# Folding a layer norm into the products behind it: mean into the weights, factor into q, k and v, with a new prologue

## What is computed

```python
def _layernorm(x, axis=-1, eps=1e-05):
    m = jnp.mean(x, axis=axis, keepdims=True)
    v = jnp.var(x, axis=axis, keepdims=True)
    return (x - m) / jnp.sqrt(v + eps)
...
q = (x @ Wq + bq).reshape(b, s, NH, HD)
k = (x @ Wk + bk).reshape(b, s, NH, HD)
v = (x @ Wv + bv).reshape(b, s, NH, HD)
q = _layernorm(q, q_scale, q_bias)
k = _layernorm(k, k_scale, k_bias)
v = _layernorm(v, v_scale, v_bias)
scores = jnp.einsum('bqhd,bkhd->bhqk', q, k) * scale
probs = jax.nn.softmax(scores, axis=-1)
out = jnp.einsum('bhqk,bkhd->bqhd', probs, v).reshape(b, s, NH * HD)
return out @ Wo + bo
...
x = x + _L0_attn_ref(_layernorm(x, axis=-1), ...)
x = x + _L0_ffn_ref(_layernorm(x, axis=-1), ...)
```

## Time and profile before

| what | value |
|---|---|
| median of 3 runs | 345.06 us (344.67 to 345.42) |
| profiled execution, device time | 344.79 us |
| its span, first to last instruction | 343.0 us |
| TensorE busy | 311.4 us (91%), 4111 records |
| ScalarE (ACT) busy | 275.7 us (80%) |
| VectorE (DVE) busy | 234.0 us (68%) |
| POOL busy | 62.1 us (18%) |
| DMA traffic | 22.86 MB, mean 67 GB/s |

### The profile page before, as it was taken

How to read it: one execution, slowest core, us unless ns; L and a number is a source line. 1 busy time by engine, 2 the same in 40 slices (tenths; PEclk the granted TensorE clock), 3 DMA queues, 4 the chain that set the end, 5 groups by cost and what they waited for, 6 DMA issues and landing times.

```text
span 343.0 us, 10532 instructions
## 1 busy us (share of the span) xinstructions
PE 311.4 (91%) x4111; PEld 145.3 (42%) x4111; DVE 234.0 (68%) x609; ACT 275.7 (80%) x315; POOL 62.1 (18%) x110
## 2 busy tenths in 40 slices
PE   7588888899999999999999999999998998989997
PEld 7484332253353424452354335443442233323576
DVE  4886788777776877688677877787846462453255
ACT  1517989989987898889988998899889998999611
POOL 6752400311003200420012200420022100020020
PEclk9969999999999999999999999999999999999999
DMA  3624104224002320323023400232022203000000
GB/s 76 188 86 155 33 2 156 80 78 124 2 33 94 98 92 2 116 69 121 0 76 99 131 0 0 92 101 84 0 97 88 97 2 102 25 2 1 34 0 31
DMA packets 22948, 22.86 MB, mean 67 GB/s; under 512 B 3200, under 2 KB 19968, under 8 KB 22912
## 3 DMA queue, kind: packets, MB, share of 16 engines
q1 hardware_dynamic: 21200, 21.23, 19.5%
q10 hardware_dynamic: 1712, 1.15, 1.1%
HBM read 13.45 MB, written 8.65 MB: 64 GB/s over the span
## 4 chain that ended last, share of the span: by engine, by line
PE 54%; ACT 22%; issue 9%; DVE 9%; DMA 2%; ACTq 1%; POOL 1%; POOLq 0%; DVEq 0%
PE oacc L911 22%; ACT probs L765 20%; PE side L835 13%; PE side L828 8%; PE scores L896 8%; ACT osb L728 1%; DMA wraw<-in_L_attn_Wv 1%; DVE x2n L1085 1%; PE scores L1002 1%; DVE ht L1161 1%; DMA kst<-parts 1%; DVE qk_sum L1144 1%; DVE ht L1160 1%; DVE hy L1162 1%; ACT th L723 1%
## 5 line engine op out<-in xcount | busy, mean ns | idle before, releaser
L765 ACT ACTIVATE probs<-scores 128x1536 f32<-128x1536 f32 (+1 forms) x256 | 248.7, 1027 | 35.9 <-PE scores L896 33.8
L911 PE MATMUL oacc<-probs,vaug 128*32 128x512 f32 x1024 | 136.4, 604 | 7.2 <-ACT osb L728 3.4
L896 PE MATMUL scores<-qst,kst 32*128 32x512 f16 x512 | 50.5, 384 | 9.8 <-ACT probs L765 7.1
L560 POOL TENSOR_SCALAR ve<-mv 128x4 f32<-128x4 f32 (+1 forms) x17 | 9.0, 528 | 219.6 <-DVE mv L1079 198.5
L911 PEld LDWEIGHTS oacc<-probs,vaug 128*32 128x32 f32 x1024 | 20.3, 108 | 39.9 <-ACT probs L765 28.9
L835 PE MATMUL side<-x2T_parts,gu_parts 128*32 128x512 f16 x504 | 35.0, 379 | 1.3 <-DVE x2T_parts L1276 1.3
L896 PEld LDWEIGHTS scores<-qst,kst 32*128 32x128 f16 x512 | 12.9, 90 | 51.8 <-ACT probs L765 39.2
L835 PEld LDWEIGHTS side<-x2T_parts,gu_parts 128*32 128x32 f16 x504 | 14.3, 96 | 32.9 <-issue 22.3
L835 PEld LDWEIGHTS side<-wqkv,xnT 128*32 128x32 f32 x736 | 21.0, 110 | 14.3 <-issue 13.8
L835 PE MATMUL side<-wqkv,xnT 128*32 128x128 f32 x736 | 24.6, 273 | 1.7 <-DVE xnT L1106 0.9
L1282 DVE SCALAR_TENSOR_TENSOR ga<-th,side 128x512 f32<-128x512 f32 x21 | 14.4, 685 | 15.5 <-ACT th L723 15.5
(11 more groups left out here) (158 smaller groups left out, 346.3 us busy)
## 6 DMA issues: line engine op xcount, KB each, us to landing
parts_dram<-parts SPq DMA_DIRECT2D x15, 256.0 KB, 2.4
qst<-parts_dram SPq DMA_DIRECT2D x15, 256.0 KB, 2.7
kst<-parts_dram SPq DMA_DIRECT2D x15, 256.0 KB, 3.0
x_in<-in_L_attn_x SPq DMA_DIRECT2D x8, 256.0 KB, 2.6
x_res<-in_L_attn_x SPq DMA_DIRECT2D x8, 256.0 KB, 3.6
parts_dram<-parts SPq DMA_DIRECT2D x15, 128.0 KB, 1.9
out_dram<-y SPq DMA_DIRECT2D x7, 256.0 KB, 2.1
parts_dram<-shift_fill SPq DMA_DIRECT2D x2, 128.0 KB, 4.7
```

The lines of the kernel that those rows point to most:

```text
L560: pool.tensor_scalar(ve[:, ts], mv[:, ts, 1], LN_EPS, None, ALU.add).then_inc(ve_done, 1)
L765: act.activation(out, src, ACT.Exp).then_inc(exp_done, 1)
L896: last = pe.matmul(scores[:, j if j < TRIPLE else TRIPLE + u % 2, :], kst[r, g, kt * P:(kt + 1) * P], qst[r, g, :], start=True, stop=True)
L911: last = pe.matmul(oacc[STRIP * j:STRIP * (j + 1), :], vaug[:, kt, NG * g + j, :], probs[:, kt, j, :], start=first, stop=last_of_half)
```

## The change

The factor of the first norm and its mean are no longer applied to x. x is loaded a second time, already transposed by the host's layout (xT), and goes into the products as it is. The mean is taken out of the weights: (I - 1/128) W, and the heads' mean as well, both by two small products on TensorE per weight with copies on ScalarE in between. The norm's factor is applied where q, k and v are read out of PSUM: four operations of 128 columns with a per-row scalar, in place of one addition of 512 columns. The xT pieces, VectorE's copy and the application are gone. FFN weights come laid out transposed, and the nine transposes with their copies are gone. Small vectors are loaded together. The head norm's root is one third-order step and one Newton step, eight chained instructions after the seed where there were nine. In the prologue, POOL's clearing of vaug and its root of v move to VectorE, v_c of sequence 0 moves behind heads_normed, 26 keep_warm matmuls stand ahead of rq, and WARM_AGAIN is 36 instead of 12.

```diff
-WARM_AGAIN = 12
+WARM_NORM = 26
+WARM_AGAIN = 36
+W_KS = ([0], [1, 2])
-SIDE = {0: ["a_v"], 1: ["a_rq"], 2: ["b_OT1", "a_rk"], 3: ["b_onT", "e_xT"], 4: ["b_Wo"], ...
+SIDE = {0: ["a_v"], 1: ["a_rq"], 2: ["b_OT1", "a_rk"], 3: ["b_onT"], 4: ["b_Wo"], ...
-FIRST_SIDE = {1: ["f_xT"], 2: ["f_q"], 3: ["f_k"], 4: ["a_v"], 6: ["e_xT"], 8: ["a_rq"], ...
+FIRST_SIDE = {1: ["f_q"], 2: ["f_k"], 4: ["a_v"], 8: ["a_rq"], 9: ["a_rk", "e_q"], 10: ["e_k"],
...
+            def load_xT(b):
+                if not (isinstance(b, int) and b == 0):
+                    wait_apart(sp, v_filled, b, passed)
+                sp.dma_start(xT[:, :], xT_d[b, :, :]).then_inc(xT_loaded, 16)
...
                 wait_apart(pool, mv_done, NT * b + tiles[-1] + 1, passed)
+                if rs is rs1:
+                    wait_apart(pool, vc_done, b, passed)
...
+            def centred_weights():
+                for n, ks in enumerate(W_STEPS):
+                    act.wait_ge(w_mean_filled, n + 1)
+                    act.activation(wT_mean_out[:, ks, :], scores[:, n, 0:len(W_KS[n]) * P], ACT.Copy)\
+                       .then_inc(w_mean_copied, 1)
+                for n, ks in enumerate(W_STEPS):
+                    act.wait_ge(w_head_filled, n + 1)
+                    act.activation(wqkv[:, ks, :], scores[:, 2 + n, 0:len(W_KS[n]) * D], ACT.Copy).then_inc(w_centred, 1)
...
+            centre_weights()
             for k, (name, turn_before) in enumerate(PROLOGUE):
-                if k == 1:
-                    pe.wait_ge(w_centred, 1)
+                if name in ("e_q", "e_k"):
+                    pe.wait_ge(w_centred, 1 + k)
                 if name == "a_rq":
-                    prepare_later_weights()
+                    keep_warm(WARM_NORM, scores[:, 0, 0:P])
                 piece(name, turn_before, occupant_in_prologue(k))
-            pe.wait_ge(wT_copied, 3)
-            keep_warm(WARM_AGAIN, scores[:, 3, 0:P])
+            keep_warm(WARM_AGAIN, scores[:, 0, 0:P])
             output_bias_product()
...
+            def scaled_with_bias(b, out, bank, bias):
+                dve.wait_ge(rs1_done, b + 1)
+                for t in range(NT):
+                    last = dve.scalar_tensor_tensor(out=out[:, t, :], in0=bank[:, t * D:(t + 1) * D],
+                                                    scalar=rs1[:, t:t + 1], in1=wqkv[:, bias, :],
+                                                    op0=ALU.mult, op1=ALU.add)
+                return last
...
                 dve.wait_ge(sem_f, b + 1)
-                dve.tensor_tensor(out=qk_c[:, w, :, :],
-                                  in0=side[:, BANK[name], :].rearrange("p (t d) -> p t d", t=NT),
-                                  in1=wqkv[:, 3 + w, :].unsqueeze(1).broadcast_to((P, NT, D)), op=ALU.add)\
-                   .then_inc(qkc_done, 1)
+                scaled_with_bias(b, qk_c[:, w, :, :], side[:, BANK[name], :], 3 + w).then_inc(qkc_done, 1)
...
+            sums_cleared()
             ln1_stats(0)
-            centre_weights()
-            ln1_apply(0)
-            copy_xT(0)
             centre_biases()
...
             heads_normed(0)
-            sums_v(0)
+            centred_v(0)
+            prepare_small()
             dve.wait_ge(qk_aff_done, 2)
             own_parts()
-            prepare_small()
+            sums_v(0)
             score_bound()
+            own_v_rsqrts()
...
```

More of the change, by code:

```diff
@@ L95 @@
 IN_SUMS = ("a_v", 0)
-PROLOGUE = [("e_xT", -2), ("e_q", -2), ("e_k", -2), ("a_v", -1), ("a_rq", -1), ("a_rk", -1)]
+PROLOGUE = [("e_q", -2), ("e_k", -2), ("a_v", -1), ("a_rq", -1), ("a_rk", -1)]
 def slots_of(phase):
@@ L523, in turn @@
                     shift_rows(i)
+                if phase in ("first", "loop", "third last"):
+                    load_xT(i + 2)
                 if phase in ("first", "loop"):
@@ L536, in _ @@
                 turn(i, "loop")
-            turn(B - 3, "near")
+            turn(B - 3, "third last")
             turn(B - 2, "near")
@@ L802, in keep_warm, with centre_weights @@
                     pe.matmul(out, ident[:, :], ident[:, :], start=True, stop=True)
-            keep_warm(WARM_UP, scores[:, 3, 0:P])
-            def prepare_later_weights():
-                for m, w in enumerate((wg_f, wu_f, wd_f)):
-                    pe.wait_ge(ints_floated, m + 1)
-                    for j in range(NF):
-                        last = pe.transpose(scores[:, m, j * P:(j + 1) * P], w[:, j, :], ident[:, :])
-                    last.then_inc(wT_filled, 1)
+            keep_warm(WARM_UP, scores[:, 4, 0:P])
+            def centre_weights():
+                pe.wait_ge(filled, 8)
+                pe.wait_ge(w_loaded, 16)
+                for n, ks in enumerate(W_KS):
+                    for c, k in enumerate(ks):
+                        last = pe.matmul(scores[:, n, c * P:(c + 1) * P], w_raw[:, k, :], mean_out[:, :],
+                                         start=True, stop=True)
+                    last.then_inc(w_mean_filled, 1)
+                for n, ks in enumerate(W_KS):
+                    pe.wait_ge(w_mean_copied, n + 1)
+                    for c, k in enumerate(ks):
+                        last = pe.matmul(scores[:, 2 + n, c * D:(c + 1) * D], wT_mean_out[:, k, :], head_mean_out[:, :],
+                                         start=True, stop=True)
+                    last.then_inc(w_head_filled, 1)
             def output_bias_product():
@@ L1150, in _ @@
             n_qk = 2 * NT * NH
-            v_all, y_all, t_all = (z[:, :, :, :].rearrange("p w t h -> p (w t h)") for z in (hv, hy, ht))
+            v_all, y_all, t_all, a_all = (z[:, :, :, :].rearrange("p w t h -> p (w t h)") for z in (hv, hy, ht, ha))
             RUN_OF_QK = slice(0, n_qk)
-            def newton_step(run, k, cols):
-                def step(ins, n):
-                    ins.then_inc(newton, 1)
-                    dve.wait_ge(newton, 8 * run + 3 * k + n)
-                v, y, t = v_all[:, cols], y_all[:, cols], t_all[:, cols]
-                step(dve.tensor_tensor(out=t, in0=y, in1=y, op=ALU.mult), 1)
-                step(dve.scalar_tensor_tensor(out=t, in0=t, scalar=-0.5, in1=v, op0=ALU.mult, op1=ALU.mult), 2)
-                last = dve.scalar_tensor_tensor(out=y, in0=t, scalar=1.5, in1=y, op0=ALU.add, op1=ALU.mult)
-                if k < 2:
-                    step(last, 3)
-                else:
-                    last.then_inc(rsqrt_done, 1)
```

298 lines of the change are left out of this document (151 added, 147 removed).

## The result

The changed kernel takes 350.44 us (median of 4 runs, 350.03 to 350.72), the kernel before 345.24 beside it (4 runs, 344.67 to 345.60). The ratio is 1.0154, with a 95% interval of 1.0136 to 1.0173: slower, as forecast, but by 5.2 us where 2.5 were forecast, and outside the range of 345.3 to 349.8. The profiled execution took 350.72 us with a span of 349.0; its own span is 6.0 above the 343.0 of before.

What follows compares the result with a forecast made beforehand. It took data to bound the prologue, a 2.0 us floor per head unit turn 0, and mostly TensorE's work turns 1 to 5. Prologue +2.3, turn 0 +1.0 and loop -0.5 on 344.8 gave 347.6 us, range 345.3 to 349.8.

Steps and rivals of the forecast that it cites:

- The prologue, +2.3 forecast: Before turn 0: fillers in TensorE's queue move first scores from 27.2 to 29.5 us, +2.3 (bounds +1.6 and +3.5).
- at 26.1: Prologue: kst's data lands near 25.6, so without the fillers the scores could start at 26.1 us.
- Turn 0, +1.0 forecast: Turn 0: VectorE's added work makes qk_n late and a_rq passes it on, +1.0 us (bounds -0.7 and +1.9).
- the collision moves with the chain: Turn 0: POOL's FFN weight splitting starts later too, so it still slows the root's first steps (1.00 against 0.26).
- the clock at 1.00 throughout: Prologue sign of being right: unbroken TensorE fillers up to about 29 us, at the full granted clock.
- The factor sets, +0.26 forecast: Reading out q, k, v: four 128-wide operations take 0.95 against 0.69 us, +0.26 each (bounds +0.17 and +0.42).
- The loop, -0.5 forecast: Turns 1 to 5: removed transposes outweigh later x2T_parts, net -0.1 us a turn, -0.5 over five.
- VectorE runs without a gap: Turns 1 to 5: two of three set additions lie between Wo and x2T_parts, making x2T_parts 0.3 us later after Wo.
- Dear instructions: Rival, chance 0.15: factor sets cost +0.42 or more each, loop turns +0.25 instead of -0.1; run 349.5 us.
- No stall in turn 0: Rival, chance 0.12: POOL's splitting falls behind the root, 1.7 us of slowed steps and the stall go; run 345.9.
- The fillers don't bind: Rival, chance 0.06: prologue fillers cost at most half of 0.224, data sets the start at 26.1; run 344.2 us.
- TensorE's work is the price of the loop: Rival, chance 0.09: each loop turn gives back 0.60 and the wait, 4.0 us over five instead of 0.5; run 344.1.

Runs made afterwards that it cites:

- first experiment: Changed kernel with 16 fillers fewer (WARM_AGAIN 20 instead of 36): 349.79 us, ratio 1.0126 to the kernel before.
- fifth run: Changed kernel with the norm's factor left out, q, k and v read out by one wide addition instead of four operations: 346.51 us, ratio 1.0046.
- second experiment: Changed kernel with POOL's splitting of the FFN weights moved ahead of turn 0: 347.16 us, ratio 1.0065.
- third experiment: Changed kernel with the statistics of x for sequence 2 placed ahead of v's centring on VectorE: 347.25 us, ratio 1.007.
- fourth experiment: Changed kernel with ten fillers put ahead of a_rq in unit 8 of turn 0, inside TensorE's wait: 348.45 us, ratio 1.0105.
- ninth run: Changed kernel with VectorE's order in loop turns changed: centring before the second part of the x2 norm, squares later: 349.27 us, ratio 1.012.
- sixth experiment: Changed kernel with three fillers added in unit 3 of every loop turn: 353.66 us, ratio 1.0256.
- twelfth: Kernel before with VectorE's order in the loop turns changed, as in the ninth run: 344.91 us, ratio 1.0008.
- seventh run: Kernel before with POOL's splitting of the FFN weights moved ahead of turn 0's part: 346.25 us, ratio 1.0038.
- eighth: Changed kernel with 16 fillers fewer, POOL's FFN weight split before turn 0 and the statistics of x ahead of v: 345.33 us, ratio 1.0012.
- eleventh run: Changed kernel with 24 fillers, POOL's early weight split, statistics ahead of v and VectorE's new loop order: 343.40 us, ratio 0.9936.
- tenth: Changed kernel with 24 fillers instead of 36, POOL's early weight split and statistics ahead of v: 344.58 us, ratio 0.999.

## Why the prediction was wrong

**The prologue, +2.3 forecast, +3.13 measured.** The mechanism was right: fillers in TensorE's own queue, not the data (first experiment). The terms were too small by a few tenths each. The first 18 fillers end at 8.54 instead of 8.1; the weight products, put at 1.5 between bounds of 1.3 and 2.5, take 1.95 (10.49 - 8.54); q, k, v and the 26 fillers with 0.23 of wait end at 19.55 instead of 18.0. From there on the count of fillers held: 20.62 + 8.20 = 28.82. The 0.45 of issue that I added behind them isn't there. That the data "would be there" for scores "at 26.1" was wrong as well: with 16 fillers fewer it was 27.8, since kst's load was issued at 24.37 and not near 23.0, and took 3.10 and not 2.55. Part of the miss is chance: the same first fillers take from 5.70 to 7.11 us in the runs of the changed kernel and its variants, and the first scores of the seven kernels with this count of fillers start at 29.38 to 30.32, with the changed kernel's the latest. My 29.5 lies inside. In six of the seven they come 21.8 us behind the start of the weight products (21.2 in the fifth run), so this chance passes straight into the time. In the kernel before it doesn't: its first fillers took 5.68 to 6.79 in three kernels, and the first scores start at 27.17 to 27.19, since TensorE waits for data behind them. The change takes that wait away. I had reckoned with the 18 fillers as the bound of q, but gave their spread no price.

**Turn 0, +1.0 forecast, +3.86 measured.** This step failed, and it is the one that put the result outside the range.
- The lateness of qk_n: 21.52 after the first scores (51.84 - 30.32), where I had said 20.4. The sums started 1.93 later and not 1.46: v's product was ready 0.19 later (10.98 after the first scores for 10.79), the set took 0.29 more (1.04 for 0.75 from start to start), and the statistics 1.45 with a gap of 0.20 among them. And the sum and root together were 0.16 longer (7.21 for 7.05), not 0.4 shorter, because "the collision moves with the chain" was not the whole of it: it grew from 1.7 to 2.4, as v's squares on POOL joined it, and that outweighed the 0.5 that the shorter chain of steps gave. I had the squares in a bound (+1.9) and left them out of the forecast. Second and third experiment. In units 8 and 9 the lateness costs 1.9 (fourth experiment).
- The clock, **1.5 us**, was in no term and in no rival; I had written of the clock for the prologue alone ("the clock at 1.00 throughout") and asked nothing of it in turn 0. Yet the rows were there: behind the 2.60 of idle time in the earlier trace rows the transposes took 1.94, and the earlier trace rows has the clock at 0.50 there. A forecast wait of 0.91 + 1.0 = 1.9 should have raised the question. In the fourth experiment fillers in the stall gave back 1.5.
- The rest is 0.4: 0.2 in units 0 to 7, where the pieces are spread otherwise, and 0.2 in unit 11, which waits 0.41 for k's dearer set and doesn't in the fifth run.

**The factor sets, +0.26 forecast, +0.43 measured.** I took the value between a start distance of 0.19 and the two-scalar operation at 0.28 each, "because there is one scalar". The far end was right: 1.12 for four, as the earlier trace rows shows for the old apply, and over the 1.1 that I had named as a sign of being wrong. The row of 0.19 was of an operation on SBUF without a tensor as a second input, and so the poorer match. The Trainium skill, VectorE: DVE Perf Modes, section "The DRAIN you can't avoid", from which I had worked out the estimate of +0.47, was nearer than my reading; this case's trace agrees with it to 0.04.

**The loop, -0.5 forecast for five turns, -0.94 measured**, but for a reason that I didn't have: 1.0 of it is the stall in turn 2, which no work of the change accounts for. Without it the turns are level, and that part of the measured time was luck for my sum. I had also read the stall as work: the 37.5 a turn from the earlier trace rows is a mean over three turns, one of which is the 38.33 with the stall; the others take 37.1 to 37.3. I had said that the removal gives up to 0.34 and that "VectorE runs without a gap" behind Wo, so that x2T_parts comes late; both are what the fifth and ninth experiments show, 0.34 each. The dear sets, at the place where they stood, made the two cancel. In the rival of dear instructions the turn was to be 0.25 longer; that was too much, because the removal was worth more than I gave it there.

**The rivals.** "Dear instructions" (0.15) had the price of a set right and gave 349.5, 0.9 under the result. That it came so near is luck: it put the loop at +1.25, where -0.94 was measured, and had neither the clock nor the larger collision. "No stall in turn 0" supposed that POOL's splitting would fall behind the root; it fell on it, and the second experiment, which takes it away, shows that the place was the right one and the price too low (3.3 us by the medians, not 1.7). "The fillers don't bind" and "TensorE's work is the price of the loop" are refuted, the first by the changed kernel's trace (36 fillers in 8.20) and the first experiment, the second by its level turns, and only in its sum: taken alone, TensorE's work in unit 3 is paid for the most part (sixth experiment), and I had expected less of it.

**What stays open.** The stall without a releaser. It is 0.86 in turn 2 of the kernel before, and 0.97 and 0.73 there in the twelfth and seventh run; it is absent from the changed kernel; it is 0.96 and 1.10 at the end of turn 1 in the two runs with 20 fillers, 0.48 with 24 and the new order. It comes and goes with edits elsewhere in TensorE's program, but in each of the six runs that have it, it stands in the first pass of TensorE's loop, which begins with turn 2: ahead of the loop's first scores (first, eighth and eleventh run) or ahead of a product of its first unit (the kernel before, seventh and twelfth). The later passes never show it. Transfers of a queue that the page calls "instruction" are seen in these stretches (two or three in 5 to 10 us), but also in the changed kernel, where TensorE doesn't stall. That TensorE waits there for its own instructions is the likely cause, and it is argued, not shown. Nor is it settled why the clock stayed low for one unit in one execution and for two in others (unit 9: 3.97 in the changed kernel, 4.97 to 5.08 in the first, sixth and ninth run), with equal waits of 2.78 and 2.79. In the changed kernel it fell at the end of the wait, in the first run before the end (48.00 to 49.00 has 0.58, and a_rq starts at 49.44), and it rose again at about 55 in both (55.00 to 56.00 has 0.93 and 1.00). The mean granted clock is 0.995 in the profiled execution of the changed kernel and 0.99 in its other three, as in the first, sixth and ninth run, so the shorter of the two is probably the rarer; no trace of the three is kept.

## What to carry to other kernels

Price a wait of an engine twice: once as lateness, and once for what the engine's clock does behind it. Here 1.9 us of added waiting cost 1.5 more, and either of two small reorderings that brought the wait from 2.8 to 1.2 was worth 3 us. When a change takes work off one engine and puts dearer instructions on another, look at what stands ahead of the instruction that the first engine waits for, and move the independent work behind it: the fold lost 5 us as it was written and gained 1.6 by the medians once the order, the count of fillers and POOL's work had been fitted to it. Fillers that end before the data arrives are free, and those that end behind it are paid one for one; so their number has to be counted again whenever the chain beside them gets shorter. A forecast that leans on a mean over several turns should look at each of them first: one may hold a stall that isn't work.

## What the runs showed of the hardware

- TensorE's granted clock stayed at 1.00 (2.4 GHz) through a wait of 1.20 and 1.25 in the two profiled executions, and was at 0.50 (1.2 GHz) behind waits of 2.01 and 2.79; at 0.50 a P.V product took 1.90 instead of 1.07.
- The first 18 fillers of the program took between 5.70 and 7.11 us where nothing about them differs. Their pace doubles at another moment in each execution, between 4.7 us (eighth run) and 7.7 us (fifth), with the first of them at 1.8 in both; the windows of the changed kernel (first row) and of the ninth run (second) have 6 and 11 of their records in the same us, while the clock column reads 1.00 in both:

```profile
6.00:7.00 1.00, 1.00 (x6) 1.00 (x6) 0.58 (x2) 0.00 (x0) 0.95 (x1) 1.00 0.76 194
```

```profile
6.00:7.00 1.00, 1.00 (x11) 1.00 (x10) 0.58 (x2) 0.00 (x0) 0.92 (x2) 1.00 0.61 119
```

  The Trainium skill, TensorE: Matmul & The Clock Gate, section "What you observe", says that the change of pace under sustained work comes at a moment that differs from run to run by half a us either way; here the moments lie 3.0 us apart, which is the measurement to go by.
- POOL and VectorE slow each other both ways. A step of the root of 0.36 takes 0.54 to 1.18 beside POOL's squares or weight split; four applications of a norm take 2.96 instead of 1.11; and POOL's own operation on 128x4 takes 1.00 instead of 0.23 beside a VectorE subtraction with two inputs in SBUF.
- A stall of TensorE of 0.5 to 1.1 us came and went with edits tens of us ahead of it (1.10 in the eighth run, none in the tenth with its four matmuls more), always in the first pass of its loop.
